# TensorE takes two tiles of the gather-convolution in one step, and VectorE copies out the turned tiles of the odd heads

## The chip, the core and the metric

The kernel runs on one core of a Trainium2 chip, as one program. The metric is the device time of that program in microseconds (us). Engines are named as in the profile: PE (TensorE matmul), PEld (TensorE weight load), ACT (ScalarE), DVE (VectorE), POOL (GpSimd), SP (SyncE, here a DMA queue).

## What is computed

Input x is 16 sequences of 512 tokens with 128 channels. A modulated layer norm gives h; an adaptive gather-convolution with 8 heads and 32 taps is added to x; a second modulated layer norm feeds a mixture of 8 experts with the best 2 chosen; its output is added to x. The change lies in the gather-convolution:

```python
wave = (x @ wave_w.T + wave_b).reshape(Bx, Lx, H, 2)
freq = MIN_FREQ + sigmoid(wave[..., 0]) * (MAX_FREQ - MIN_FREQ)
phase = tanh(wave[..., 1]) * freq
offs = phase[..., None] + freq[..., None] * taps
pos = clip(arange(Lx)[None, :, None, None] + offs, 0.0, Lx - 1)
...
gathered = g0 + frac[..., None] * (g1 - g0)
kmat = (x @ kernel_w.T + kernel_b).reshape(Bx, Lx, H, K)
bins = clip(floor((offs + MAX_RECEPTIVE) / (2.0 * MAX_RECEPTIVE) * K), 0, K - 1)
w = take_along_axis(kmat, bins, axis=3)
y = einsum('blhs,blhsd->blhd', w, gathered).reshape(Bx, Lx, Cx)
```

## The kernel before, in words

**Tiling.** Sequences are taken in 8 pairs (i). In each pair there are 8 rounds (r), one for each residue of the token modulo 8, and in a round 8 heads (h). One head of one round is a tile T of 128 tokens by 512 grid points, so there are 64 rounds (R) and 512 tiles (NT). The kernel does not gather. For each token and each grid point a tile holds a count of taps, got from three matmuls with 32 rows of weights and a relu; it is multiplied by the kernel value of its bin, turned, and multiplied by differences of h.

**One tile, step by step.**
- TensorE, `gap_on` (line 985): a 32-row matmul into `ps_s[T % 4]`. The 32 rows are those of head `T % 4`; four such row groups lie side by side in the array.
- ScalarE, `gap` (line 775): relu on the bank, in place.
- TensorE, `tile_on` (line 990), then `undone_on` (line 994): two more 32-row matmuls added onto the same bank.
- VectorE, `weighted` (line 1303): maximum and product, from the bank into `aw[T % 3]`.
- TensorE, `turn_tile` (line 1000): four 128x128 transposes into one of two banks `ps_t`.
- ScalarE, `tile_evicted` (line 783): copy of that bank to `att[h]`.
- TensorE, `weigh` (line 1020): 32 matmuls on four heads' `att`, twice a round.

**Two banks, one order.** Everything that is turned goes through the two banks `ps_t` in one fixed order, `ORDER` (line 41): the tiles, one `count` a round after head 0, two `edge` units after heads 2 and 4, and in some rounds after heads 6 and 7 the turned h, parameters, steps or second-norm rows. Unit u uses bank `u % 2`, so `unit` (line 891) makes TensorE wait until unit u-2 has been copied out:

```python
u = UNIT[tag]
...
if u >= 2:
    pe.wait_ge(s_ev, u - 1)
return ps_t[u % 2]
```

**The order of work** is written out by hand, one in-order queue for each engine. In the loop over T, TensorE issues `undone_on(T+1)`, `tile_on(T+2)`, `gap_on(T+3)`, then `turn_tile(T)`, then what belongs to the head: `counts` (h 0), `weigh` of the round before (h 1), `turn_edges` (h 2 and 4, line 1007), `bins` (h 3, line 946), `weigh` (h 5), `weigh_edges` (h 7, line 1030), and once in a pair of sequences `waves`, `scores` (line 1052), `ranks` (h 0) and `outputs` (line 1042; h 0 in round 6, h 6 in round 0). ScalarE issues `gap(T+3)`, `tile_evicted(T)`, then its own things for the head: `counted` (h 0, line 767), `edge_evicted` (h 2 and 4, line 790), `copied` (h 3, line 798), and in rounds 1 and 2 the four normalising activations of `centred` (h 1 and 3, line 735). VectorE issues `weighted(T)`, then `edge_terms` (h 2), `binned` (h 5, line 1287) and the norms' and choices' work. `gap_on` waits until VectorE has read tile T-4 out of its bank.

**After the loop** come the last scores and ranks, the scatter of rows to experts, the experts' matmuls (lines 1138 to 1159) and the sums. The change does not touch them.

Of the kernel before, what the change touches and what calls it, by code (L numbers as in the profile page):

```python
# [7 lines left out]
RES = 8  # L8
# [5 lines left out]
NT = PAIRS * TILES  # L14
# [5 lines left out]
ROWS = 32  # L20
QUAD = P // ROWS
KRING = 4
RING = 3
BANKS = 4
SCALE = 2.0 ** 27
GATE = 2.0 ** 90
# [52 lines left out]
UNIT = {tag: n for n, tag in enumerate(ORDER)}  # L79
SIDES = side_order()  # L80
SIDE = {tag: n for n, tag in enumerate(SIDES)}
SLOTS = HEADS + 2
HALF = HEADS // QUAD

# [6 lines left out]
def build(nc, x, wave_wT, wave_b, kern_wT, kern_b, out_wT, w12T, w3T, gateT, cT, wmod,  # L91
# [23 lines left out]
    with ctx:  # L115
# [6 lines left out]
        def sem(name):  # L122
            return ctx.enter_context(nc.semaphore(name))
# [139 lines left out]
        s_kf = sem("end_terms_set")  # L263
        s_n, s_p, s_e = sem("count_added"), sem("gap_product"), sem("gap_ready")
        s_aw, s_at, s_ev, s_y, s_yy = sem("weighted"), sem("turned"), sem("evicted"), sem("y_product"), sem("y_copied")
        s_ga, s_ow, s_xo, s_gc, s_sc = sem("gains_loaded"), sem("out_weights_scaled"), sem("x_new"), sem("h2_ready"), sem("scores_read")
        s_oh, s_gd, s_tg, s_gate = (sem("choice_masks"), sem("score_gap"), sem("gap_tanh"),
                                           sem("gates_in_rows"))
# [224 lines left out]
        def _(pool):  # L493
# [95 lines left out]

            def h_steps(i):  # L590

                pool.wait_ge(s_ev, UNIT["ht", i, 1] + 1)
                if i:
                    pool.wait_ge(s_at, UNIT["dl", i - 1, 1] + 1)
                q = i % 2
                pool.tensor_tensor(dt[:, :, 0:RES - 1, :].rearrange("p b r t -> p r b t"), ht[:, q, 0:RES - 1, :].rearrange("p r (b t) -> p r b t", b=2),
                                   ht[:, q, 1:RES, :].rearrange("p r (b t) -> p r b t", b=2), ALU.subtract)
                pool.tensor_tensor(dt[:, :, RES - 1, 0:HP - 1], rows(ht[:, q, RES - 1, 0:1], [[HP, 2], [1, HP - 1]]),
                                   rows(ht[:, q, 0, 1:2], [[HP, 2], [1, HP - 1]]), ALU.subtract).then_inc(s_dt, 1)
# [109 lines left out]
        def _(act):  # L709
# [93 lines left out]
            for n in range(4):  # L803
                params_turned(0, n)
            counted(0)
            for T in range(BANKS - 1):
                gap(T)
            for b in range(2):
                steps_turned(0, b)
            for T in range(NT):  # L810
                i, R, r, h = T // TILES, T // HEADS, T // HEADS % RES, T % HEADS
                last, more = i - 1, i + 1 < PAIRS
                if T + BANKS - 1 < NT:
                    gap(T + BANKS - 1)
                tile_evicted(T)
                if h == 0 and R + 1 < NR:
                    counted(R + 1)
                if h == 2:
                    edge_evicted(R, 0)
                if h == 3 and R:  # L820
                    copied(R - 1)
                if h == 4:
                    edge_evicted(R, 1)
                if i:
                    if (r, h) in ((2, 1), (2, 3)):
                        centred(1, last, h // 2)
                    if r == 3 and h >= 6:
                        h2_turned(last, h - 6)
                    if (r, h) == (4, 5):
                        gap_tanh(last)  # L830
                if more:
                    if (r, h) in ((1, 1), (1, 3)):
                        centred(0, i + 1, h // 2)
                    if r == 2 and h >= 6:
                        h_turned(i + 1, h - 6)
                    if (r, h) == (3, 3):
                        waves(i + 1)
                    if r == 4 and h >= 6:
                        params_turned(i + 1, h - 6)
                    if r == 5 and h >= 6:  # L840
                        params_turned(i + 1, h - 4)
                    if r == 6 and h >= 6:
                        steps_turned(i + 1, h - 6)
# [34 lines left out]
        def _(pe):  # L878
# [12 lines left out]
            def unit(*tag):  # L891

                u = UNIT[tag]
                assert u == issued[0], (tag, ORDER[issued[0]])
                issued[0] += 1
                if u >= 2:
                    pe.wait_ge(s_ev, u - 1)
                return ps_t[u % 2]

            def aside(*tag):  # L900
# [32 lines left out]
                last.then_inc(s_at, 1)  # L933

            def waves(i):
                pe.wait_ge(s_ev, UNIT["ht", i, 1] + 1)
                bank = aside("wave", i)
                for r in range(RES):
                    last = nc.tensor.matmul(bank[:, r * 16:r * 16 + 16], ht[:, i % 2, r, :], ww[:, :], start=True, stop=True)
                last.then_inc(s_sd, 1)  # L940
# [26 lines left out]
            def counts(R):  # L967
                i, r = R // RES, R % RES
                if r == 0:
                    pe.wait_ge(s_ev, UNIT["ptt", i, 3] + 1)  # L970
                bank = unit("count", R)
                for g in range(2):
                    last = nc.tensor.matmul(bank[:, g * QUAD * EDGES:(g + 1) * QUAD * EDGES], ptt[:, i % 2, 2 * r + g, :], ce[:, :], start=True, stop=True)
                last.then_inc(s_at, 1)
# [12 lines left out]
            def tile_on(T):  # L987
                pe.wait_ge(s_e, T + 1)
                at, params = strip(T)
                nc.tensor.matmul(ps_s[T % BANKS][:, :], params, cn[at, 0, :], start=False, stop=False, skip_group_check=True)  # L990
# [17 lines left out]
                last.then_inc(s_at, 1)  # L1008

            def weigh(R, g):  # L1010
                pe.wait_ge(s_ev, UNIT["tile", HEADS * R + QUAD * g + QUAD - 1] + 1)
                if g == 0:
                    if R % RES == 0:
                        pe.wait_ge(s_ev, UNIT["dl", R // RES, 1] + 1)
                    if R:
                        pe.wait_ge(s_yy, R)
                for j in range(NJ):
                    for k in range(QUAD):
                        h = QUAD * g + k
                        last = nc.tensor.matmul(ps_y[ROWS * k:ROWS * k + ROWS, g * P:g * P + P], dl[:, R // RES % 2, j, h, :],  # L1020
                                                att[:, h, j * P:j * P + P], start=(g == 0 and j == 0), stop=(g == HALF - 1 and j == NJ - 1))
                last.then_inc(s_y, 1)

            def weigh_edges(R, g):
                pe.wait_ge(s_ev, UNIT["edge", R, g] + 1)
                if R % RES == 0 and g == 0:
                    pe.wait_ge(s_hld, 16 * 3 * (R // RES + 1))
                for k in range(QUAD):
                    o = R % RES * 2 * C + QUAD * g + k
                    last = nc.tensor.matmul(ps_y[ROWS * k:ROWS * k + ROWS, g * P:g * P + P], rows(hgr[:, R // RES % 2, o:o + 1], [[HEADS, 2 * D]]),  # L1030
                                            att[:, HEADS + g, k * P:k * P + P], start=False, stop=False)
                last.then_inc(s_y, 1)
# [11 lines left out]
                last.then_inc(s_sd, 1)  # L1044

            def scores(i):
                pe.wait_ge(s_ev, UNIT["h2", i, 1] + 1)
                if i == 0:
                    pe.wait_ge(s_late, NLATE)
                bank = aside("gate", i)  # L1050
                for r in range(RES):
                    last = nc.tensor.matmul(bank[:, r * 8:r * 8 + 8], h2t[:, r, :], gw[:, :], start=True, stop=True)  # L1052
                last.then_inc(s_sd, 1)
# [16 lines left out]
            for n in range(4):  # L1070
                params_turned(0, n)
            counts(0)
            for T in range(BANKS - 1):
                gap_on(T)
            tile_on(0)
            undone_on(0)
            tile_on(1)
            for b in range(2):
                steps_turned(0, b)
            for T in range(NT):  # L1080
                i, R, r, h = T // TILES, T // HEADS, T // HEADS % RES, T % HEADS
                last, more = i - 1, i + 1 < PAIRS
                if T + 1 < NT:
                    undone_on(T + 1)
                if T + 2 < NT:
                    tile_on(T + 2)
                if T + BANKS - 1 < NT:
                    gap_on(T + BANKS - 1)
                turn_tile(T)
                if h == 0 and R + 1 < NR:  # L1090
                    counts(R + 1)
# [90 lines left out]
        def _(dve):  # L1182
# [107 lines left out]
            def weighted(T):  # L1290
# [13 lines left out]
                                                             rows(ks[:, R % 2, h, o:o + 1], [[0, b - a], [1, HP]]), ALU.max, ALU.mult)  # L1304
                ins.then_inc(s_aw, 1)

            def edge_terms(R):

                dve.wait_ge(s_ev, UNIT["count", R] + 1)
                dve.wait_ge(s_kd, R + 1)  # L1310
                if R >= 2:
                    dve.wait_ge(s_est[R % 2], 32 * (R // 2))
                nc.vector.scalar_tensor_tensor(kr[:, R % 2, :], en[:, R % 2, :], -TAPS / 2 * SCALE, kd[:, R % 2, :], ALU.add, ALU.mult).then_inc(s_kr, 1)
# [38 lines left out]
            binned(0)  # L1352
            binned(1)
            edge_terms(0)
            for T in range(NT):
                i, R, r, h = T // TILES, T // HEADS, T // HEADS % RES, T % HEADS
                last, more = i - 1, i + 1 < PAIRS
                weighted(T)
                if h == 2 and R + 1 < NR:
                    edge_terms(R + 1)  # L1360
                if h == 5 and R + 2 < NR:
# [196 lines left out]
```

## Time and profile before

| | |
|---|---|
| median of 3 runs | 1334.32 us |
| runs, lowest to highest | 1331.52 to 1336.67 us |
| the profiled execution's own time | 1336.08 us |
| its span, first to last instruction | 1334.0 us |
| mean granted TensorE clock | 0.956 of full speed |
| busy over the span | PE 86%, PEld 56%, DVE 53%, ACT 69%, POOL 44% |
| the loop over tiles, first to last turned tile | 40.9 to 965.0 us |

The loop over tiles is some 924 of 1334 us; the experts follow from about 1022 us to 1285 us. In the loop the time of a round repeats to a few hundredths of a microsecond, so single pairs of tiles can be read off the timeline and multiplied. Busy time of a matmul is modelled and overlaps the next one; the start of an instruction is what to read. The chain of waits that ended last has little of the loop among its largest parts, so the loop is read from the waits and the timeline.

### The profile page before, as it was taken

To read this page: it belongs to the slowest core of one execution; us is meant where nothing else is said; L and a number is where in the kernel's file an instruction comes from. 1 tells how busy PE (TensorE), PEld (TensorE's weight loads), DVE (VectorE), ACT (ScalarE), POOL (GpSimd) and SP (SyncE) were. 2 spreads that over 40 slices of the span, in tenths; PEclk is the share of its full clock that TensorE was granted. 3 is DMA by queue.
4 is the path that set the end of the run, shared out by engine and by line. 5 is a ranking of instruction groups with operands and counts; after the bars stand their busy time and mean duration, and the time that the engine had idled before them with its cause. 6 is when DMAs were issued, how large, how long until landed. Compare 5 with 4: busy or idle time off the path is not lost. (4 is left out here: it accounts for less than half of the span.)

```text
span 1334.0 us, 34820 instructions
## 1 busy us (share of the span) xinstructions
PE 1141.6 (86%) x11855; PEld 741.1 (56%) x11855; DVE 702.3 (53%) x2252; ACT 916.3 (69%) x1906; POOL 588.1 (44%) x838
## 2 busy tenths in 40 slices
PE   5699999999999999999999999999922989999840
PEld 2366656656665665666566566656621656556520
DVE  4345655564665656566565656556551333333336
ACT  2488887888888788878878888887700555555520
POOL 4133155346436435633643563442436554545520
PEclk9899999999999999999999999999955999999975
DMA  5546446445645544554554455444412442222237
GB/s 181 156 123 175 112 144 162 136 134 165 156 124 167 163 125 140 168 144 121 168 162 127 143 151 138 143 140 116 150 64 68 138 133 72 71 71 71 68 138 262
DMA packets 213178, 179.81 MB, mean 135 GB/s; under 512 B 147600, under 2 KB 183184, under 8 KB 212368
## 3 DMA queue, kind: packets, MB, share of 16 engines
q1 hardware_dynamic: 204336, 159.68, 42.5%
q0 software_dynamic: 8672, 17.92, 4.1%
q8 instruction: 100, 1.64, 0.5%
q14 instruction: 70, 0.57, 0.2%
HBM read 95.42 MB, written 82.12 MB: 133 GB/s over the span
## 5 line engine op out<-in xcount | busy, mean ns | idle before, releaser
L1303 DVE SCALAR_TENSOR_TENSOR aw<-ps,ks 128x64 f32<-128x64 f32 (+7 forms) x960 | 382.0, 437 | 387.4 <-PE ps L994 342.8
L775 ACT ACTIVATE ps<-ps,f 128x512 f32<-128x512 f32 x512 | 343.4, 671 | 131.2 <-PE ps L985 131.2
L1000 PE MATMUL ps<-ident,aw 128*128 128x128 f32 x2048 | 332.9, 285 | 31.6 <-ACT att L783 15.9
L783 ACT ACTIVATE att<-ps 128x512 f32<-128x512 f32 x512 | 310.2, 606 | 11.5 <-PE ps L1000 11.2
L1000 PEld LDWEIGHTS ps<-ident,aw 128*128 128x128 f32 x2048 | 216.3, 141 | 157.9 <-issue 134.4
L604 POOL COPY kn<-kn 128x256 f32<-128x256 f32 x64 | 25.4, 397 | 436.8 <-DVE kn L1287 436.8
L990 PE MATMUL ps<-cn,ptt 32*128 32x512 bf16 x512 | 198.8, 388 | 13.9 <-ACT ps L775 13.9
L994 PE MATMUL ps<-cn,ptt 32*128 32x512 bf16 x512 | 198.7, 388 | 0.0
L985 PE MATMUL ps<-cp,ptt 32*128 32x512 bf16 x512 | 197.9, 389 | 0.0
L705 POOL DMA_INDIRECT y_scratch<-aw,idu x135 | 129.3, 958 | 129.4 <-ACT aw L866 128.1
L853 ACT ACTIVATE ee<-ps 128x256 f32<-128x256 f32 x135 | 51.9, 385 | 152.8 <-PE ps L1144 152.8
L573 POOL DMA_INDIRECT slot_scratch<-hrow,spotu x128 | 127.3, 995 | 48.2 <-issue 33.4
L1144 PE MATMUL ps<-kn,ee 128*128 x270 | 143.0, 612 | 0.0
L1020 PE MATMUL ps<-att,dl 128*32 128x128 f32 x4096 | 140.0, 278 | 0.1
L1450 DVE TENSOR_TENSOR aw<-ee,ps 128x256 f32<-128x256 f32 x135 | 56.9, 421 | 136.4 <-ACT ee L853 135.5
L1020 PEld LDWEIGHTS ps<-att,dl 128*32 128x32 f32 x4096 | 105.1, 110 | 22.2 <-ACT att L790 10.6
L994 PEld LDWEIGHTS ps<-cn,ptt 32*128 32x128 bf16 x512 | 46.4, 91 | 124.6 <-issue 121.2
L1138 PE MATMUL ps<-ident,dl 128*128 128x128 f32 x135 | 38.3, 283 | 55.0 <-DMA dl<-slot_scratch 32.7
L1007 PE MATMUL ps<-ident,ka 128*128 128x128 f32 x512 | 77.3, 274 | 7.8 <-POOL ka L617 7.8
L790 ACT ACTIVATE att<-ps 128x512 f32<-128x512 f32 x128 | 77.9, 608 | 8.3 <-PE ps L1007 8.3
L1159 PE MATMUL ps<-hgr,aw 128*128 x540 | 82.5, 275 | 0.1
L1151 PEld LDWEIGHTS ps<-ident,aw 128*128 128x128 f32 x270 | 38.0, 141 | 71.6 <-issue 46.4
(176 smaller groups left out, 1652.1 us busy)
## 6 DMA issues: line engine op xcount, KB each, us to landing
k_scratch<-kn SPq DMA_DIRECT2D x64, 512.0 KB, 3.5
ka<-e_scratch SPq DMA_DIRECT2D x64, 512.0 KB, 3.2
ks<-k_scratch SPq DMA_DIRECT2D x128, 130.0 KB, 3.3
e_scratch<-kr SPq DMA_DIRECT2D x128, 126.0 KB, 3.4
dl<-slot_scratch SPq DMA_DIRECT2D x135, 65.0 KB, 1.8
att<-y_scratch SPq DMA_DIRECT2D x16, 512.0 KB, 5.2
xc<-in_x SPq DMA_DIRECT2D x8, 512.0 KB, 5.9
h_scratch<-hx SPq DMA_DIRECT2D x16, 256.0 KB, 4.2
```

What stands on the lines that cost most here:

```text
L573: pool.indirect_dma_start(out=slots[:, :], out_offset=bass.IndirectOffsetOnAxis(ap=spotu[:, k * RES + r:k * RES + r + 1], axis=0), in_=hro ...
L705: pool.indirect_dma_start(out=yscr[:, :], out_offset=bass.IndirectOffsetOnAxis(ap=idu[:, s:s + 1], axis=0), in_=yrow[:, y, :], in_offset=N ...
L775: act.activation(ps_s[T % BANKS][:, :], ps_s[T % BANKS][:, :], ACT.Relu, scale=f27[:, i % 2, r, h:h + 1]).then_inc(s_e, 1)
L783: act.activation(att[:, h, :], ps_t[UNIT["tile", T] % 2][:, :], ACT.Copy).then_inc(s_ev, 1)
L985: nc.tensor.matmul(ps_s[T % BANKS][:, :], params, cp[at, :], start=True, stop=True).then_inc(s_p, 1)
L990: nc.tensor.matmul(ps_s[T % BANKS][:, :], params, cn[at, 0, :], start=False, stop=False, skip_group_check=True)
L994: nc.tensor.matmul(ps_s[T % BANKS][:, :], params, cn[at, 1, :], start=False, stop=True, skip_group_check=True).then_inc(s_n, 1)
L1000: last = nc.tensor.transpose(bank[:, j * P:j * P + P], aw[:, T % RING, j * P:j * P + P], ident[:, :])
L1020: last = nc.tensor.matmul(ps_y[ROWS * k:ROWS * k + ROWS, g * P:g * P + P], dl[:, R // RES % 2, j, h, :], att[:, h, j * P:j * P + P], start ...
L1144: nc.tensor.matmul(ps_h[j % 2][:, :], xT[:, j % 2, :], w12[:, bass.ds(experts[j % 8] * (2 * FF), 2 * FF)], start=True, stop=True).then_inc ...
L1159: last = nc.tensor.matmul(ps_z[j % 2][:, 0:C], hidT[:, j % 2, k * P:k * P + P], w3[:, bass.ds(experts[j % 8] * (HALVES * C) + k * C, C)], ...
L1303: ins = nc.vector.scalar_tensor_tensor(dst[:, a:b, :], src[:, a:b, :], -TAPS * SCALE, rows(ks[:, R % 2, h, o:o + 1], [[0, b - a], [1, HP]] ...
```

## The change

TensorE's step covers two tiles. At each even head it issues `tile_on` for T+2 and T+3, `gap_on` for T+4 and T+5, `undone_on` for T+2 and T+3; `turn_tile` and what belongs to a head stay at their heads. ScalarE issues `gap(T+4)` and `gap(T+5)` at each even head ahead of `tile_evicted(T)`, and copies out even heads alone. VectorE issues `weighted(T+2)` in step T, and after it, at odd heads, a copy of the turned tile T to `att[h]`, counted on a semaphore of its own. `aw` has four buffers in place of three. The number of instructions is the same. Who has copied out which unit is kept in the table `EVICTION`, and every wait that asked for a unit's copy now asks for its entry there.

```diff
-RING = 3
+RING = 4
...
+def by_vector(tag):
+
+    return tag[0] == "tile" and tag[1] % 2 == 1
+
+
+def evictions():
+
+    done, counts = [0, 0], {}
+    for tag in ORDER:
+        k = by_vector(tag)
+        done[k] += 1
+        counts[tag] = done[k]
+    return counts
+
+
+EVICTION = evictions()
...
-            for T in range(BANKS - 1):
+            for T in range(BANKS):
                 gap(T)
...
-                if T + BANKS - 1 < NT:
-                    gap(T + BANKS - 1)
-                tile_evicted(T)
+                if h % 2 == 0 and T + BANKS < NT:
+                    gap(T + BANKS)
+                    gap(T + BANKS + 1)
+                if h % 2 == 0:
+                    tile_evicted(T)
...
                 if u >= 2:
-                    pe.wait_ge(s_ev, u - 1)
+                    old = ORDER[u - 2]
+                    pe.wait_ge(s_dv if by_vector(old) else s_ev, EVICTION[old])
...
-                pe.wait_ge(s_ev, UNIT["tile", HEADS * R + QUAD * g + QUAD - 1] + 1)
+                pe.wait_ge(s_ev, EVICTION["tile", HEADS * R + QUAD * g + QUAD - 2])
+                pe.wait_ge(s_dv, EVICTION["tile", HEADS * R + QUAD * g + QUAD - 1])
...
-            for T in range(BANKS - 1):
+            for T in range(BANKS):
                 gap_on(T)
-            tile_on(0)
-            undone_on(0)
-            tile_on(1)
+            for T in range(2):
+                tile_on(T)
+            for T in range(2):
+                undone_on(T)
...
-                if T + 1 < NT:
-                    undone_on(T + 1)
-                if T + 2 < NT:
+                if h % 2 == 0 and T + 2 < NT:
                     tile_on(T + 2)
-                if T + BANKS - 1 < NT:
-                    gap_on(T + BANKS - 1)
+                    tile_on(T + 3)
+                    if T + BANKS < NT:
+                        gap_on(T + BANKS)
+                        gap_on(T + BANKS + 1)
+                    undone_on(T + 2)
+                    undone_on(T + 3)
                 turn_tile(T)
...
+            def tile_evicted(T):
+
+                R, h = T // HEADS, T % HEADS
+                dve.wait_ge(s_at, UNIT["tile", T] + 1)
+                if R:
+                    dve.wait_ge(s_y, weighed(R - 1, "tile", h // QUAD))
+                nc.vector.tensor_copy(att[:, h, :], ps_t[UNIT["tile", T] % 2][:, :]).then_inc(s_dv, 1)
...
+            for T in range(2):
+                weighted(T)
             for T in range(NT):
...
-                weighted(T)
+                if T + 2 < NT:
+                    weighted(T + 2)
+                if h % 2:
+                    tile_evicted(T)
```

## Rows read from the trace of the kernel before

**Rows 1.** The page: busy time, and the clock granted to TensorE in 40 slices.
```profile
PE 1141.6 (86%) x11855; PEld 741.1 (56%) x11855; DVE 702.3 (53%) x2252; ACT 916.3 (69%) x1906; POOL 588.1 (44%) x838
...
PEclk9899999999999999999999999999955999999975
```

**Rows 2.** Waits, 100 to 1000 us: engine line, releaser, us, times, longest.
```profile
DVE aw L1303 <- PE ps L994: 321.3, 307, 2.5
...
PE ps L1000 <- ACT att L783: 15.3, 72, 0.2
```

**Rows 3.** Timeline, heads 0 and 1 of a plain round: start us, us, engine line.
```profile
870.83 0.39 PE L994 MATMUL ps<-cn,ptt 32*128 32x512 bf16 x1
...
871.15 0.42 PEld L1000 LDWEIGHTS ps<-ident,aw 128*128 128x128 f32 x4 [0.23 <-issue]
...
871.30 0.66 ACT L775 ACTIVATE ps<-ps,f 128x512 f32<-128x512 f32 x1 [0.34 <-PE ps L985]
...
871.88 0.59 ACT L783 ACTIVATE att<-ps 128x512 f32<-128x512 f32 x1
...
872.36 0.59 ACT L767 ACTIVATE en<-ps 128x504 int32<-128x504 f32 x1
...
872.58 0.42 PEld L1000 LDWEIGHTS ps<-ident,aw 128*128 128x128 f32 x4 [0.48 <-issue]
```

**Rows 4.** Timeline, heads 2 and 3 of the same round.
```profile
874.19 0.39 PE L994 MATMUL ps<-cn,ptt 32*128 32x512 bf16 x1
...
875.94 0.42 PEld L1000 LDWEIGHTS ps<-ident,aw 128*128 128x128 f32 x4 [0.31 <-issue]
...
877.39 0.39 PE L994 MATMUL ps<-cn,ptt 32*128 32x512 bf16 x1
```

**Rows 5.** Timeline, heads 6 and 7 of the same round, no extra units.
```profile
880.75 0.38 PE L994 MATMUL ps<-cn,ptt 32*128 32x512 bf16 x1
...
882.25 0.42 PEld L1000 LDWEIGHTS ps<-ident,aw 128*128 128x128 f32 x4 [0.23 <-issue]
...
883.44 0.39 PE L994 MATMUL ps<-cn,ptt 32*128 32x512 bf16 x1
```

**Rows 6.** Timeline, heads 6 and 7 of a round with extra units.
```profile
491.32 0.39 PE L994 MATMUL ps<-cn,ptt 32*128 32x512 bf16 x1
...
493.07 0.42 PEld L1000 LDWEIGHTS ps<-ident,aw 128*128 128x128 f32 x4 [0.31 <-issue]
...
494.86 0.38 PE L994 MATMUL ps<-cn,ptt 32*128 32x512 bf16 x1
```

**Rows 7.** Timeline, heads 0 and 1 of a round with scores at head 0.
```profile
451.08 0.39 PE L994 MATMUL ps<-cn,ptt 32*128 32x512 bf16 x1
...
452.11 1.85 PE L1052 MATMUL ps<-gw,h2t 128*128 128x8 f32 x16
...
455.82 0.39 PE L994 MATMUL ps<-cn,ptt 32*128 32x512 bf16 x1
```

**Rows 8.** Timeline, heads 2 and 3 of a round with normalising activations.
```profile
539.96 0.38 PE L994 MATMUL ps<-cn,ptt 32*128 32x512 bf16 x1
...
543.94 0.38 PE L994 MATMUL ps<-cn,ptt 32*128 32x512 bf16 x1
...
544.03 1.69 ACT L735 ACTIVATE hrow<-xo,shift,rstd 128x128 f32<-128x128 f32 x4
```

**Rows 9.** Busy by stretch: heads 4 and 5 of that round; a stretch after scores.
```profile
543.94:548.50 4.56, 3.69 (x51) 2.37 (x51) 2.10 (x5) 4.40 (x10) 2.72 (x4) 1.00 0.57 217
...
570.00:573.00 3.00, 3.00 (x42) 2.09 (x39) 2.27 (x13) 1.26 (x2) 1.07 (x1) 0.53 0.62 112
```

**Rows 10.** Timeline, the same matmul at half the clock.
```profile
572.81 0.60 PE L994 MATMUL ps<-cn,ptt 32*128 32x512 bf16 x1
```

**Rows 11.** Timeline, VectorE: a sum out of PSUM, and `weighted`.
```profile
870.46 0.68 DVE L1320 TENSOR_TENSOR xo<-ps,xc 128x512 f32<-128x512 f32 x1
...
874.61 0.76 DVE L1303 SCALAR_TENSOR_TENSOR aw<-ps,ks 128x64 f32<-128x64 f32 x2 [0.88 <-PE ps L994]
```

More of the change, by code:

```diff
@@ L265, in build @@
         s_aw, s_at, s_ev, s_y, s_yy = sem("weighted"), sem("turned"), sem("evicted"), sem("y_product"), sem("y_copied")
+        s_dv = sem("tile_evicted_by_vector")
         s_ga, s_ow, s_xo, s_gc, s_sc = sem("gains_loaded"), sem("out_weights_scaled"), sem("x_new"), sem("h2_ready"), sem("scores_read")
@@ L590, in h_steps @@
             def h_steps(i):
-                pool.wait_ge(s_ev, UNIT["ht", i, 1] + 1)
+                pool.wait_ge(s_ev, EVICTION["ht", i, 1])
                 if i:
@@ L935, in waves @@
             def waves(i):
-                pe.wait_ge(s_ev, UNIT["ht", i, 1] + 1)
+                pe.wait_ge(s_ev, EVICTION["ht", i, 1])
                 bank = aside("wave", i)
@@ L969, in counts @@
                 if r == 0:
-                    pe.wait_ge(s_ev, UNIT["ptt", i, 3] + 1)
+                    pe.wait_ge(s_ev, EVICTION["ptt", i, 3])
                 bank = unit("count", R)
@@ L1010, in weigh @@
             def weigh(R, g):
-                pe.wait_ge(s_ev, UNIT["tile", HEADS * R + QUAD * g + QUAD - 1] + 1)
+                pe.wait_ge(s_ev, EVICTION["tile", HEADS * R + QUAD * g + QUAD - 2])
+                pe.wait_ge(s_dv, EVICTION["tile", HEADS * R + QUAD * g + QUAD - 1])
                 if g == 0:
                     if R % RES == 0:
-                        pe.wait_ge(s_ev, UNIT["dl", R // RES, 1] + 1)
+                        pe.wait_ge(s_ev, EVICTION["dl", R // RES, 1])
                     if R:
@@ L1024, in weigh_edges @@
             def weigh_edges(R, g):
-                pe.wait_ge(s_ev, UNIT["edge", R, g] + 1)
+                pe.wait_ge(s_ev, EVICTION["edge", R, g])
                 if R % RES == 0 and g == 0:
@@ L1046, in scores @@
             def scores(i):
-                pe.wait_ge(s_ev, UNIT["h2", i, 1] + 1)
+                pe.wait_ge(s_ev, EVICTION["h2", i, 1])
                 if i == 0:
@@ L1305, in weighted @@
                 ins.then_inc(s_aw, 1)
+            def tile_evicted(T):
[4 more added lines that the diff above has]
+                nc.vector.tensor_copy(att[:, h, :], ps_t[UNIT["tile", T] % 2][:, :]).then_inc(s_dv, 1)
             def edge_terms(R):
-                dve.wait_ge(s_ev, UNIT["count", R] + 1)
+                dve.wait_ge(s_ev, EVICTION["count", R])
                 dve.wait_ge(s_kd, R + 1)
```

## The prediction, made before the changed kernel had run

> **What bounds the kernel now.** First the page [rows 1]: TensorE is the busiest engine, 86% of the span, and in the loop its granted clock is full. That looks like a loop bound by TensorE alone, but busy time of matmuls is modelled, so the waits come next [rows 2]. VectorE waits 321.3 us of the loop for TensorE; TensorE hardly records waits for the copies (15.3 us). Then the timeline of one plain round, which shows how near those copies are.
>
> Take heads 0 and 1 [rows 3] and count from the moment the three 32-row matmuls start. Tile 0 is turned at +0.32. ScalarE's relu starts at +0.47, its copy of tile 0 0.58 later, at +1.05, and lasts 0.59, to +1.64. Tile 1 is turned at +1.75, 0.11 after that. Between tile 0 and tile 1 only `count` goes through the two banks, so tile 1 needs tile 0's bank. The idle ahead of tile 1's loads is 0.48 where it was 0.23 ahead of tile 0's: TensorE already waits 0.25 there. The pair is over at +3.36 [rows 3, 4], 1.61 behind tile 1's turning. Heads 2 and 3 are alike [rows 4]: tile 3 at +1.75, end at +3.20. An `edge` unit makes tile 3 use tile 2's bank, and in the same way tile 5 uses tile 4's. Between tiles 6 and 7 nothing goes through the banks in a plain round: tile 7 needs tile 5's bank, long free, and the pair takes 2.69 [rows 5].
>
> So the loop is bound by a chain through two engines: strips, relu, copy, next turning.
>
> **What the change does to that chain.** In an even step ScalarE now has two relus ahead of the copy of tile T, and that copy is still ScalarE's, since T is even. The relus cannot run earlier, as their `gap_on` matmuls are issued in the same step. VectorE's new copies are those of odd tiles, which do not hold these three turnings.
>
> Step by step: relu T+4 at +0.47, relu T+5 at +1.05, copy at +1.63, its end at +2.22, tile T+1 turned at +2.33. That is 1.75 plus 0.58. What follows (1.61 for heads 0, 1 and 4, 5; 1.45 for heads 2, 3) is unchanged, so **each such pair grows by 0.58**. The distance from one relu to the next is not in the trace: below, 0.48, as from a copy to ScalarE's next operation [rows 3]; above, 0.66, a whole relu. I take 0.58, the distance from a relu to a copy, as the relu is what it times.
>
> TensorE's own work shrinks. Two blocks of strips with 0.32 each become one. In it `tile_on` and `gap_on` cover four row groups and `undone_on` comes a second time to two of them, so it costs one more stream: 0.22, the difference between this matmul at half and at full clock, 0.60 and 0.38 [rows 5, 10]. The block takes 0.54 (bounds 0.32, all six side by side, and 0.64, nothing gained). Where TensorE sets the time this and one lost switch from strips to full-height matmuls (idle 0.23 [rows 3]) matter; where ScalarE's copy sets it, they are swallowed by the wait.
>
> **Heads 6 and 7, plain.** Tile 7 is not held. 0.54 of strips, 0.42 for the loads of four transposes, and the 1.19 behind tile 7's turning [rows 5] make 2.15 where 2.69 was: **0.54 less**. The next `gap_on` needs VectorE: its first product starts 0.42 behind a strip [rows 4, 11], here at +0.64, and two of 0.76 end at +2.16. That is just in time, so there is nothing more to gain.
>
> **Heads 6 and 7 with extra units** (turned h, parameters, steps, second norm; rounds 2 to 6). An extra unit stands between tiles 6 and 7, which makes tile 7 wait for tile 6's copy by ScalarE: +1.75 now [rows 6], +2.33 then, and 1.79 behind it: 4.12 for 3.54, **0.58 more**.
>
> **Pairs with long work at head 0** (waves, scores, outputs) or outputs at head 6. TensorE sets these: scores alone take 1.85, more than ScalarE's chain needs, and the pair 4.74 [rows 7]. They lose 0.10 of strips and some 0.2 of a switch: **0.3 less**.
>
> **Rounds 1 and 2, normalising activations.** These four activations (1.69 [rows 8]) make the next relu late, so those pairs are long now: 3.98 [rows 8] at heads 2, 3 and 4.56 [rows 9] at heads 4, 5. Their delay fits into the time ScalarE will then wait: behind the `count` copy at +2.11 they begin at +2.6 and end at +4.3, before the next relu is due (3.94 plus 0.47). Heads 2, 3 come to 3.78: 0.2 less. Behind head 3 there is `copied` ahead of them; they end about 0.3 after the relu is due at 3.78 plus 0.47, so heads 4, 5 come to some 4.2: 0.4 less.
>
> **VectorE's copies.** 128x512 out of PSUM by VectorE is not in the trace. ScalarE's copy (0.59) and VectorE's sum out of PSUM (0.68 [rows 11]) bound it; I take 0.65. It waits for turning T+1 (+2.33 and about 0.66 for the last transpose), runs to +3.65, and the next `weighted` is ready only at 3.94 plus 0.64. It hides, with 0.9 to spare. Banks that wait for it (`edge`, `count`, extra units) come 0.9 or more later. The fourth `aw` buffer keeps `weighted(T+2)` from waiting for a turning; it costs nothing. No DMA is added, and SP and POOL, which follow the products' semaphores, keep their order.
>
> **The sum.** Of the 256 pairs of tiles, by the conditions in the code: 128 are held by ScalarE's copy and plain (41 at heads 0, 1; 47 at 2, 3; 40 at 4, 5), 128 x 0.58 = +74.2. 35 with extra units, +20.3. 21 plain at heads 6, 7, -11.3. 29 with long work, -8.7. 14 and 14 behind normalising activations, -2.8 and -5.6. The other 15 (start, choices in round 4, last sequences) at zero. In all **+66 us**. The profiled execution took 1336.08 us, 1.8 above the median of the runs; the sum there is 1402, and against the median 1334.3 + 66 = **1400 us**, slower by 5%.
>
> **Rivals.**
>
> *TensorE's saving comes through (faster).* It is one mechanism: VectorE shares the copies, ScalarE is lighter by 256 copies, and no turning waits. For it speaks that ScalarE is the second busiest engine [rows 1]. Every pair would then lose what a plain last pair loses: 256 x 0.54 = 138, 1196 us. It decides if tile T's copy is over before TensorE reaches tile T+1, at about +1.4. Against it stands the order: the copy cannot start before +1.05 even if the second relu cost nothing, and ends at +1.64. I give it 0.05. The Trainium skill, TensorEngine Tiling (Array Packing), section PSUM Bottleneck, advises to use both ScalarE and VectorE to empty PSUM; by that rule alone the time would be this rival's. It speaks of throughput, and the trace here shows a latency.
>
> *The clock drops.* TensorE's own work in a held pair is some 3.0 of 3.94, 76%. The nearest row is the pair at heads 4, 5 of a normalising round, 3.69 busy of 4.56, 81%, at clock 1.00 [rows 9]. But after scores, whose matmuls stream 8 columns each, the clock was 0.53 [rows 9]. If a quarter of the pairs ran at half the clock with 2.0 more each, that is 64 x 2.0 = 128: 1530 us. I give it 0.08. The Trainium skill, TensorE: Matmul & The Clock Gate, section "A second HAM failure mode: psum-queue depth-cycling", tells of a kernel whose small idle spells between groups on changing banks made the clock swing; by it this rival would be likely. In this trace small waits have not done it.
>
> *VectorE becomes late.* A copy that waits at the head of its queue keeps the next product back. It decides if the copy ends later than 4.58, 0.9 more than worked out. With 0.3 lost in each of 192 pairs that gives 58 more, 1460 us. 0.04.
>
> *No change that can be measured.* A measurement of this kernel tells about 0.5%, 7 us. It would take a distance between relus near 0.15, against every row: 0.03.
>
> **How the numbers follow.** Forecast 0.80. Relu to relu 0.48 to 0.66 moves 163 pairs by -16 to +13; the block of strips -11 to +5 in the 50 pairs that TensorE sets; four row groups at once may bring the first relu up to one stream, 0.22, later in 163 pairs: +36. That is 1373 to 1454; with the odd pairs, and as the three will not all fall on one side, the range is 1365 to 1445. Faster 0.05, within 0.5% 0.03, slower 0.92.
>
> **What would show it.** In a plain round: TensorE's second turning at +2.33 at heads 0, 2 and 4, and an idle of about 0.9 ahead of it, laid to ScalarE's copy (line 783's successor); TensorE's recorded waits for that copy up from 15 us to over 100; rounds near 13.8 where 12.6 was; the last pair at 2.15. I am wrong if the two relus stand closer than 0.45, if the clock in the loop is below 0.95, or if most of TensorE's idle time is laid to VectorE.

## The result, and the profile after

The changed kernel took 1409.3 us (median of 4 runs, 1408.7 to 1410.2) beside 1335.0 us for the kernel before: 1.0555 times as long, interval 1.0541 to 1.0569. Forecast were 1400 us and a range of 1365 to 1445. All times here and below are of undisturbed runs, which in the last variant leaves out one of four, of 2109 us.

The page of the changed kernel: engines' busy time, and the clock granted to TensorE in 40 slices.

```profile
PE 1094.2 (78%) x11855; PEld 716.3 (51%) x11855; DVE 860.3 (61%) x2508; ACT 790.2 (56%) x1650; POOL 589.0 (42%) x838
...
PEclk9999999999999999999999999999985899999985
```

Against [rows 1] ScalarE's work has moved to VectorE (ACT 69% to 56%, DVE 53% to 61%), TensorE's share fell from 86% to 78%, and the mean clock stayed where it was (0.956 before, 0.959 now). No engine is fuller than TensorE was, and yet the kernel is slower: a matter of waits.

Its waits from 100 to 1000 us: who waited for whom, us in total, times, longest.

```profile
PEld ps L1022 <- DVE aw L1329: 163.8, 167, 1.6
...
PE ps L1022 <- ACT att L802: 141.5, 181, 1.4
...
DVE aw L1329 <- PE ps L1016: 95.9, 120, 1.8
```

Line 1022 is the turning of a tile, 802 ScalarE's copy, 1329 `weighted`. TensorE's matmuls waited 15.3 us for that copy before [rows 2] and wait 141.5 us now. The weight loads of the same turnings are put down to VectorE (163.8 us), which is the releaser that the profile happens to find for the load. The timeline settles which it is. Heads 0 and 1, then 2 and 3, of a round (start us, us, engine line; VectorE's one row here is the products of tiles 2 and 3):

```profile
420.29 0.39 PE L1012 MATMUL ps<-cn,ptt 32*128 32x512 bf16 x2
...
420.30 0.75 PE L1007 MATMUL ps<-cp,ptt 32*128 32x512 bf16 x2
...
420.73 1.24 ACT L794 ACTIVATE ps<-ps,f 128x512 f32<-128x512 f32 x2 [0.41 <-PE ps L1007]
...
421.13 1.28 DVE L1329 SCALAR_TENSOR_TENSOR aw<-ps,ks 128x512 f32<-128x512 f32 x2
...
421.88 0.60 ACT L802 ACTIVATE att<-ps 128x512 f32<-128x512 f32 x1
...
422.36 0.60 ACT L786 ACTIVATE en<-ps 128x504 int32<-128x504 f32 x1
...
422.63 0.63 PE L1022 MATMUL ps<-ident,aw 128*128 128x128 f32 x4 [0.77 <-ACT att L802]
...
424.20 0.39 PE L1012 MATMUL ps<-cn,ptt 32*128 32x512 bf16 x2
...
424.42 0.38 PE L1016 MATMUL ps<-cn,ptt 32*128 32x512 bf16 x2
...
424.63 1.24 ACT L794 ACTIVATE ps<-ps,f 128x512 f32<-128x512 f32 x2 [1.67 <-PE ps L1007]
...
425.79 0.60 ACT L802 ACTIVATE att<-ps 128x512 f32<-128x512 f32 x1
...
426.53 0.63 PE L1022 MATMUL ps<-ident,aw 128*128 128x128 f32 x4 [0.71 <-ACT att L802]
...
427.95 0.39 PE L1012 MATMUL ps<-cn,ptt 32*128 32x512 bf16 x2
```

In the first pair the two relus start at 420.73 and the copy of tile 0 only at 421.88, 1.15 behind the first relu where it was 0.58 behind before [rows 3]. Tile 1 is turned at 422.63, 0.15 after that copy ends. In the second pair the strips start at 424.20, tile 3's matmuls at 426.53, and the pair ends at 427.95: 3.75 where [rows 4] had 3.20. VectorE's product of tile 3 was over at 422.41, four microseconds before its turning, so it did not hold it; ScalarE's copy of tile 2, over at 426.39, did. `undone_on` (line 1016) starts 0.22 behind `tile_on` (line 1012), the one stream expected.

The pair at heads 6 and 7 of another round, with extra units, by the same view:

```profile
463.21 0.39 PE L1012 MATMUL ps<-cn,ptt 32*128 32x512 bf16 x2
...
465.52 0.42 PEld L1022 LDWEIGHTS ps<-ident,aw 128*128 128x128 f32 x4 [0.92 <-DVE aw L1329]
465.55 0.63 PE L1022 MATMUL ps<-ident,aw 128*128 128x128 f32 x4 [0.71 <-ACT att L802]
...
467.30 0.39 PE L1012 MATMUL ps<-cn,ptt 32*128 32x512 bf16 x2
```

The second turning is at +2.31 and the pair lasts 4.09, where [rows 6] had +1.75 and 3.54. Here the load's idle is laid to VectorE and the matmul's to ScalarE, 0.03 apart: the same wait.

One thing more, which no mean over the loop shows: the granted clock fell to half in four short stretches of the loop. Three of them are in round 2, the fourth in round 5 of the last sequences. Round 2 of two pairs of sequences, first without such a stretch, then with it (the third number from the end is the clock), and the row that stands ahead of the second:

```profile
458.00:460.50 2.50, 2.28 (x16) 0.97 (x14) 1.80 (x5) 2.50 (x8) 1.27 (x1) 1.00 0.52 98
583.00:585.50 2.50, 2.50 (x10) 0.99 (x10) 0.69 (x1) 2.40 (x6) 1.60 (x2) 0.50 0.54 103
```

```profile
582.16 0.81 PE L1029 MATMUL ps<-ident,ka 128*128 128x128 f32 x4 [1.58 <-POOL ka L636]
```

In both TensorE had just waited 1.58 for GpSimd's part of the edge unit. Experiment 4 says where that wait comes from.

### The profile page after: what moved, and what is told of

Same layout as the page of the kernel before. It is cut to its first block, busy times and chain, and to the rows that moved or that the text cites. A ratio compares the mean times of both kernels' runs of the same rounds, so it can differ in the third digit from the quotient of the medians.

```text
span 1408.1 us, 34896 instructions
## 1 busy us (share of the span) xinstructions
PE 1094.2 (78%) x11855; PEld 716.3 (51%) x11855; DVE 860.3 (61%) x2508; ACT 790.2 (56%) x1650; POOL 589.0 (42%) x838
## 4 chain that ended last, share of the span: by engine, by line
PE 54%; ACT 16%; issue 15%; POOL 7%; DVE 4%; DMA 3%; SPq 1%; POOLq 0%; DVEq 0%; ACTq 0%
PE ps L1022 12%; PE ps L1043 9%; PE ps L1170 8%; ACT att L802 7%; ACT ps L794 6%; PE ps L1012 5%; PE ps L1185 4%; PE ps L968 3%; PE ps L1053 2%; PE ps L1065 2%; PE ps L1177 2%; DMA att<-y_scratch 2%; PE ps L1164 1%; POOL y_scratch L724 1%; POOL rstd L534 1%
## 5 line engine op out<-in xcount | busy, mean ns | idle before, releaser
L794 ACT ACTIVATE ps<-ps,f 128x512 f32<-128x512 f32 x512 | 317.3, 658 | 292.5 <-PE ps L1007 292.4
L1022 PE MATMUL ps<-ident,aw 128*128 128x128 f32 x2048 | 327.9, 285 | 153.9 <-ACT att L802 152.4
L1329 DVE SCALAR_TENSOR_TENSOR aw<-ps,ks 128x64 f32<-128x64 f32 (+7 forms) x960 | 366.8, 433 | 130.7 <-PE ps L1016 105.8
L1339 DVE COPY att<-ps 128x512 f32<-128x512 f32 x256 | 176.3, 689 | 173.6 <-PE ps L1022 172.9
L802 ACT ACTIVATE att<-ps 128x512 f32<-128x512 f32 x256 | 153.3, 599 | 3.7 <-issue 1.9
L1007 PE MATMUL ps<-cp,ptt 32*128 32x512 bf16 x512 | 106.0, 391 | 4.7 <-DVE aw L1329 4.7
L1012 PE MATMUL ps<-cn,ptt 32*128 32x512 bf16 x512 | 101.4, 390 | 0.7 <-ACT ps L794 0.7
L1016 PE MATMUL ps<-cn,ptt 32*128 32x512 bf16 x512 | 98.1, 378 | 0.0
L809 ACT ACTIVATE att<-ps 128x512 f32<-128x512 f32 x128 | 77.8, 608 | 10.6 <-PE ps L1029 10.6
```

Of the source, the lines that this page charges most:

```text
L794: act.activation(ps_s[T % BANKS][:, :], ps_s[T % BANKS][:, :], ACT.Relu, scale=f27[:, i % 2, r, h:h + 1]).then_inc(s_e, 1)
L802: act.activation(att[:, h, :], ps_t[UNIT["tile", T] % 2][:, :], ACT.Copy).then_inc(s_ev, 1)
L1007: nc.tensor.matmul(ps_s[T % BANKS][:, :], params, cp[at, :], start=True, stop=True).then_inc(s_p, 1)
L1022: last = nc.tensor.transpose(bank[:, j * P:j * P + P], aw[:, T % RING, j * P:j * P + P], ident[:, :])
L1329: ins = nc.vector.scalar_tensor_tensor(dst[:, a:b, :], src[:, a:b, :], -TAPS * SCALE, rows(ks[:, R % 2, h, o:o + 1], [[0, b - a], [1, HP]] ...
L1339: nc.vector.tensor_copy(att[:, h, :], ps_t[UNIT["tile", T] % 2][:, :]).then_inc(s_dv, 1)
```

## The experiments

All are compared with the kernel before, measured on the same chip in the same sitting (medians 1334 to 1336 us). The changed kernel was timed in a sitting of its own. A pair of tiles is counted from its block of strips to the next one, a round from the block at its head 0 to that of the next round; the eight pairs of sequences are numbered from 0.

**Theory.** In 163 of 256 pairs of tiles the turning of tile T+1 waits for ScalarE's copy of tile T; the second relu stands ahead of that copy and is paid in full. **Rivals.** VectorE's copies hold the loop; a step of two tiles costs TensorE something by itself; the loop pays for ScalarE's load, not for its order.

**1. The copy between the relus.**

```diff
-                if h % 2 == 0 and T + BANKS < NT:
-                    gap(T + BANKS)
-                    gap(T + BANKS + 1)
                 if h % 2 == 0:
+                    if T + BANKS < NT:
+                        gap(T + BANKS)
                     tile_evicted(T)
+                    if T + BANKS < NT:
+                        gap(T + BANKS + 1)
```

> The changed kernel with ScalarE's order in an even step made relu T+4, copy of tile T, relu T+5 (before this: both relus, then the copy). Theory (the second relu ahead of the copy holds the turning of T+1): the copy starts at +1.24, when tile T has been turned, and the second turning comes at +1.95 where it was +2.3; held pairs fall from 3.91 and 3.76 to about 3.55 and 3.4, the pair with extra units from 4.09 to 3.7, the plain last pair grows from 2.16 to about 2.4 as the late relu now holds the next strips. 163 x -0.36 and 21 x +0.27 give -53: about 1356 us. Rival (VectorE's copies hold the loop): unchanged, 1409. Rival (a step of two tiles costs by itself on TensorE): unchanged, 1409.

Measured: 1358.3 us, ratio 1.0176 (1.0159 to 1.0193). Moving one ScalarE instruction gives back 51 of the 74 us. Plain held pairs fall to 3.54 and 3.39, as expected; the last pair stays at 2.16, where 2.4 was expected. One held pair (heads 6 and 7 of round 4, with extra units), strips, relu, copy, relu, turning, next strips:

```profile
472.79 0.39 PE L1013 MATMUL ps<-cn,ptt 32*128 32x512 bf16 x2
...
473.23 0.66 ACT L794 ACTIVATE ps<-ps,f 128x512 f32<-128x512 f32 x1 [0.99 <-PE ps L1008]
...
474.02 0.60 ACT L802 ACTIVATE att<-ps 128x512 f32<-128x512 f32 x1
...
474.51 0.66 ACT L794 ACTIVATE ps<-ps,f 128x512 f32<-128x512 f32 x1
...
474.73 0.42 PEld L1023 LDWEIGHTS ps<-ident,aw 128*128 128x128 f32 x4 [0.70 <-issue]
...
476.26 0.39 PE L1013 MATMUL ps<-cn,ptt 32*128 32x512 bf16 x2
```

The copy is at +1.23, the turning at +1.94, and the pair takes 3.47 where the changed kernel has 3.83. Both rivals that said 1409 are out as the main cause.

**2. The pairs kept, all copies by ScalarE.** The same with `by_vector` false for every tile and `tile_evicted(T)` by ScalarE at each head.

> The changed kernel, but ScalarE copies out all tiles again, the odd ones after the even ones; step of two tiles kept. Theory: held pairs stay at 3.91 and 3.76, since the copy of T stands where it stood; the normalising activations of rounds 1 and 2 start later by a copy and delay 28 pairs by 0.8 to 1.3 each: 1425 to 1440 us. Rival (VectorE's copies are the cost): back to 1350 or below.

Measured: 1426.2 us, 1.0687 (1.0669 to 1.0705). The step of two tiles does the harm without VectorE; VectorE's copies are worth 17 us in it, nearly all beside the normalising activations (12.4 in round 1 and 3.6 in round 2, added up from the two traces). Plain held pairs are at 3.91 and 3.76, as in the changed kernel.

**3. A step of one tile, odd tiles by VectorE.** The order of the kernel before on TensorE and ScalarE; VectorE issues `weighted(T+1)`, then its copy of an odd tile T.

> The kernel before with its step of one tile, but VectorE copies out the odd tiles (aw with four buffers, VectorE one tile ahead of its copy). Theory: held pairs as before, 3.36 and 3.20, as tile T's copy keeps one relu ahead of it; only pairs behind the normalising activations gain, 14 x 0.7 and 14 x 0.9: 1313 to 1325 us, faster than the kernel before. Rival (VectorE's copies are the cost): slower than 1335.

Measured: 1360.7 us, 1.0200 (1.0172 to 1.0228), **a miss**, slower where a gain was expected. Plain pairs at heads 0 to 5 are as expected and round 1 gains 0.96 us (14.70 to 13.74). But round 4 loses 2.1 to 3.6 (0.9 in pair 4 of sequences, where the kernel before has a stretch at half the clock), round 5 0.2 to 1.5 and round 2 0.7 to 1.5; over the traces that is 14.3, 5.1 and 6.3 us, against 6.5 gained in round 1; the last pair of round 7, 3.20 for 2.69, loses 3.5 more. In round 4 VectorE has the experts' choices to make. Its row there, with the turning that waits, then the next turning:

```profile
470.58 0.75 DVE L1325 SCALAR_TENSOR_TENSOR aw<-ps,ks 128x256 f32<-128x256 f32 x2
...
471.25 0.68 DVE L1335 COPY att<-ps 128x512 f32<-128x512 f32 x1
...
471.85 0.68 DVE L1309 TENSOR_TENSOR kn<-ps,kbias 128x512 f32<-128x512 f32 x1
...
473.44 0.96 DVE L1378 TENSOR_TENSOR both<-oh 128x64 bf16<-128x64 f32 x1
474.32 1.40 DVE L1325 SCALAR_TENSOR_TENSOR aw<-ps,ks 128x256 f32<-128x256 f32 x4
...
475.12 0.42 PEld L1021 LDWEIGHTS ps<-ident,aw 128*128 128x128 f32 x4 [2.53 <-DVE aw L1325]
475.12 0.66 PE L1021 MATMUL ps<-ident,aw 128*128 128x128 f32 x4 [2.23 <-DVE aw L1325]
...
477.81 1.11 PE L1021 MATMUL ps<-ident,aw 128*128 128x128 f32 x4
```

Copy, bias add and masks (up to line 1378) stand in one row ahead of the next product, and TensorE's matmuls wait 2.2 us, its loads 2.5. In the kernel before, the same turning waited for VectorE too, 0.74 and 1.03. The next four transposes take 1.11 where these took 0.66. The clock says why (second stretch; the third number from the end is the granted clock):

```profile
474.00:477.00 3.00, 1.88 (x23) 1.31 (x24) 2.42 (x6) 0.00 (x0) 0.89 (x4) 0.80 0.68 239
477.00:479.00 2.00, 2.00 (x13) 1.24 (x11) 0.76 (x2) 1.28 (x3) 0.00 (x0) 0.50 0.51 172
```

After the wait TensorE ran at half the clock, 1.2 GHz, until the next round had begun. So VectorE's copies are not free. In the step of two tiles they cost nothing in rounds 4 and 5, which take 16.03 and 15.56 with them (the changed kernel) and without them (experiment 2).

**4. VectorE's bias add ahead of its copy.** In the changed kernel, `binned(R + 2)` at head 5 moved before `tile_evicted(T)`.

> The changed kernel with VectorE's bias add of the kernel values (binned, head 5) put ahead of its copy of tile 5. Theory: in round 2 the turning of the first edge unit waits for GpSimd, whose row of work starts with that add, now behind a copy that waits for a turning; heads 2 and 3 of round 2 fall from 4.65 toward 3.76 and nothing else moves: 7 x 0.9, so 1402 to 1404 us. Rival (the round-2 wait comes from elsewhere): unchanged, 1409.

Measured: 1394.9 us, 1.0447 (1.0430 to 1.0465). Right in kind, short in size: 14 us, not 6. Round 2 falls from 17.21 to 15.83 in pairs 1, 2 and 3 of sequences (heads 2 and 3 from 4.66 to 3.76, heads 4 and 5 from 4.56 to 4.07), and from 18.20 to 15.83 in pairs 4, 5 and 6, where heads 2 and 3 had taken 6.1 to 6.2 with the half clock. Round 5 of the last sequences, the fourth place of half clock, gives 1.7 back. No stretch of this run's loop is at half the clock. The row of waits in the changed kernel, from VectorE's copy to TensorE's edge unit:

```profile
447.02 0.69 DVE L1339 COPY att<-ps 128x512 f32<-128x512 f32 x1 [0.30 <-PE ps L1022]
447.63 0.68 DVE L1313 TENSOR_TENSOR kn<-ps,kbias 128x512 f32<-128x512 f32 x1
...
448.38 0.40 POOL L623 COPY kn<-kn 128x256 f32<-128x256 f32 x1 [5.52 <-DVE kn L1313]
...
456.03 0.68 POOL L636 TENSOR_SCALAR ka<-kn 128x8 f32<-128x8 f32 x1
...
456.76 0.42 PEld L1029 LDWEIGHTS ps<-ident,ka 128*128 128x128 f32 x4 [1.82 <-POOL ka L636]
```

The copy waits for a turning, the bias add for the copy, GpSimd for the bias add, and GpSimd's operation for the edge unit stands behind the inverse deviations and half a norm, all in one queue. TensorE pays nine microseconds later.

**5 and 6. A small operation ahead of the copy, and behind it.**

```diff
                 if h % 2 == 0:
+                    act.activation(extra[:, T // 2 % 8, :], ident[:, 0:64], ACT.Copy)
                     tile_evicted(T)
```

> The changed kernel with one small ScalarE copy (128x64, SBUF to a buffer of its own) more in each even step, between the second relu and the copy of tile T. Theory (whatever stands on ScalarE between the relus and the copy is paid in full in the 163 held pairs): with some 0.2 us for such an operation each held pair grows by 0.2, from 3.91 to 4.1 and 3.76 to 3.95; the plain last pair stays at 2.16: +33, about 1442 us. Rival (ScalarE's copy is waited for but TensorE or VectorE is the bound): less than a third of it.

> The same small ScalarE copy put behind the copy of tile T. Theory: ScalarE has room there, nothing moves but the pairs behind the normalising activations: 1409 to 1415 us. Rival (the loop pays for ScalarE's load, not for its order): the same +33 as with the operation ahead of the copy.

Measured: ahead 1432.1 us, 1.0735 (1.0716 to 1.0755), so 23 us more than the changed kernel; behind 1407.8 us, 1.0549 (1.0530 to 1.0568), so nothing. The operation lasts 0.25 but moves the next one by 0.15, and held pairs grow by just that, 3.91 to 4.05 and 3.75 to 3.90. That 163 x 0.15 is 24 is in part luck: in the trace 186 pairs grow, by 26.5 us together, and some 5 come back because neither of these two runs has the changed kernel's stretches of half clock. The size expected was off by my 0.2. ScalarE does the same work in both, so its load is not what is paid: the place is.

**7. The turning first.** TensorE turns tile T ahead of the strips, ScalarE copies it ahead of both relus, VectorE adds the bias ahead of its copy.

```diff
+                turn_tile(T)
                 if h % 2 == 0 and T + 2 < NT:
                     tile_on(T + 2)
...
-                turn_tile(T)
...
-                if h % 2 == 0 and T + BANKS < NT:
-                    gap(T + BANKS)
-                    gap(T + BANKS + 1)
                 if h % 2 == 0:
                     tile_evicted(T)
+                    if T + BANKS < NT:
+                        gap(T + BANKS)
+                        gap(T + BANKS + 1)
```

> Step of two tiles, but TensorE turns tile T ahead of the strips, ScalarE copies it ahead of both relus, and VectorE's bias add stands ahead of its copy of tile 5. Theory: tile T's copy is over at about +1.4, before TensorE comes to tile T+1 at +1.5, so no turning waits: plain pairs 3.13, 3.03, 3.2 and 2.31, a plain round 11.7 where the kernel before had 12.6; less in rounds 4 and 5, where VectorE has the choices to make: 1270 to 1300 us, faster than both kernels. Rival (pairs cost by themselves, or VectorE's copies do): slower than 1335.

Measured: 1340.1 us (ten runs, 1336.5 to 1350.9; the trace is of one at 1336.5), 1.0066 (1.0037 to 1.0095). The plain pairs are near what was worked out, 3.04, 3.05, 3.16 and 2.31, and a plain round takes 11.6 us, 1.0 less than before. The total is **a miss**: rounds 2, 4 and 5 are long (up to 16.2, 17.3 and 15.1, where the kernel before has 15.4, 15.4 and 13.3), those that experiment 3 had made long. They and the pairs behind long work take the whole gain. Some 11 us of it are the clock's: four rounds 2 and four rounds 5 hold a stretch at half the clock, behind a wait of 1.8 to 2.0 us, and take 16.2 and 15.1 where the others take 15.0 and 13.6.

**8. The turning first, all copies by ScalarE.**

> As the kernel with the turning first, but ScalarE copies out all tiles. Theory: ScalarE then has two relus and two copies in a pair of some 3.1 and still keeps tile T's copy first, so plain rounds stay near 11.7 to 12; VectorE's choices in rounds 4 and 5 cost less, normalising activations in rounds 1 and 2 more: 1270 to 1310 us. If VectorE's copies are worth having it is slower than the one beside it.

Measured: 1319.8 us, 0.9894 (0.9876 to 0.9912), **faster than both kernels**, by 1.1% than the one before, but outside the 1270 to 1310 expected. Plain rounds stay at 11.56; beside experiment 7, round 4 takes 15.6 for 17.3 and round 5 13.7 for 13.6 or 15.1; round 1, beside the normalising activations, 14.0 for 13.0. From 60 us on its loop has no stretch at half the clock. Waits, 100 to 940 us:

```profile
ACT att L802 <- PE ps L1021: 117.2, 185, 1.8
...
PE ps L1021 <- ACT att L802: 17.0, 28, 1.2
```

Now ScalarE waits for the turning; the turning's matmuls wait for ScalarE's copy 17.0 us, where the changed kernel has 141.5 up to 1000 us. The whole gain is 15 us, far from 64 rounds at 1.0: against the kernel before, heads 2 and 3 lose 0.5 to 0.9 in rounds 3 to 6, and rounds 3 to 6 gain nothing as a whole.

**9 and 10. VectorE's copies only where ScalarE is full.** `by_vector` true for odd heads of round 1; then for heads 1 and 3 of rounds 1 and 2.

> As the kernel with the turning first and all copies by ScalarE, but in round 1 of each pair of sequences, where ScalarE has eight normalising activations, VectorE copies the odd tiles. Theory (a copy belongs on the engine that has time in that round): round 1 falls from 14.0 to 13.05, as in the kernel whose odd copies are all VectorE's, and the other rounds stay: 7 x 0.97 less, about 1313 us. Rival (the order alone made the gain, the engine does not matter): 1320.

> As before, but VectorE copies the tiles of heads 1 and 3 alone, in rounds 1 and 2, those directly ahead of ScalarE's normalising activations. Theory: round 1 at 13.05 to 13.3 and round 2 some 0.3 to 1.0 shorter than 14.3, with no copy of VectorE's ahead of its bias add at head 5: 1307 to 1313 us. Rival (VectorE's copies in round 2 make GpSimd's row of work late again): 1315 to 1325.

Measured: 1318.2 us, 0.9867 (0.9848 to 0.9886), and 1316.8 us, 0.9848 (0.9824 to 0.9872). **Both expectations were missed**; the second time lies in its rival's range. Round 1 falls from 14.0 to 13.04 as expected. But round 2 rises from 15.12 to 15.6 (three pairs of sequences) or 16.2 to 16.3 (three) in the first variant, and to 16.2 or 16.3 in two of six in the second. The rival's wait is there: in round 2 the edge unit waits 2.0 us for GpSimd, where it waited 1.5 in experiment 8. And the rounds of 16.2 and 16.3 are exactly those where the clock was at half behind that wait. The first variant, just behind the wait, in a pair of sequences without and in one with half clock:

```profile
419.00:421.50 2.50, 2.50 (x19) 1.38 (x18) 0.24 (x2) 2.50 (x7) 1.75 (x2) 1.00 0.54 103
305.00:307.50 2.50, 2.50 (x7) 1.02 (x6) 0.00 (x0) 2.41 (x7) 1.25 (x1) 0.50 0.50 97
```

The interval of the first variant overlaps that of experiment 8, from which it is not told apart, and that of the second variant.

## Why the prediction was right

The time was inside the range, 9 us above the forecast. The mechanism, ScalarE's second relu ahead of the copy that holds the next turning, is shown by experiments 1, 5 and 6. By its own steps:

- **The held pairs** (+0.58): measured 3.91, 3.76 and 3.91 for 3.36, 3.20 and 3.36, so +0.55, and 4.09 for 3.54 with extra units. The distance between relus, assumed, is 0.58: the copy comes 1.16 behind the first relu. The 0.03 less is the first relu, at +0.43 where it was at +0.47. A round of three such pairs and a plain last pair takes 13.73 for 12.61, near the 13.8 forecast.
- **Extra units in round 4** (+0.58) **failed**: in six pairs of sequences this last pair took 3.83, for 4.07 in most of them, so it became shorter by 0.24. The forecast added 0.58 to all 35 such pairs as if each took the 3.54 of [rows 6]. In round 4 the pair was held by VectorE, whose choices made a product late: the loads of tile 6's turning waited 1.03 for it. In the changed kernel the products are made two tiles ahead and that wait is gone.
- **The plain last pair** (-0.54): 2.16 for 2.69. The second stream of `undone_on` starts 0.22 behind, and four row groups at once delay the first relu by nothing; the upper bound on that was not needed.
- **Long work at head 0** (-0.3): 4.53 for 4.74, so -0.2; outputs at head 6 4.26 for 4.38, -0.1. A little over-priced.
- **Pairs beside the normalising activations** (-0.2 and -0.4): round 1 as forecast (3.76 for 4.04, 4.14 for 4.62). **Round 2 failed**: at heads 2 and 3 4.66 for 3.98, and 6.1 to 6.2 in the three pairs of sequences with half clock; at heads 4 and 5 4.56, unchanged, and 4.0 to 4.1 in those three. The step that failed is the sentence on VectorE's copies, "It hides, with 0.9 to spare", and that POOL keeps its order. The order holds, but I asked only whether the next product is late and not what else stands behind the waiting copy. That is the bias add that starts GpSimd's row of work. Experiment 4 prices it at 14 us, the half clock behind the wait included.
- **The sum is near in part by luck.** Added up pair by pair, the loop grew by 74.4 us between the two traces, where the terms forecast 66.1. Heads 2 to 5 of round 2 grew by 6.8 where -4.2 was forecast, 11.0 too much; the 35 pairs with extra units grew by 14.6, where 20.3 was forecast, most of the difference in round 4. These two errors have opposite signs; what is left of all other terms is 3.
- **The clock**: 0.959 over the span, 0.99 from 100 to 1034 us, so above the 0.95 that would have shown the forecast wrong. TensorE's waits of 0.7 to 0.9 in each pair did not halve it, and a quarter of the pairs at half clock, which was the rival, did not come. But the clock did fall to half in four short stretches (two before the change, in round 4), three of them right behind a wait of 1.58 for the edge unit. They cost some 1.0 us in each of those three rounds (18.2 for 17.2) and 1.5 in the fourth place (6.39 for 4.90 in experiment 4), 4 to 5 us in all. The Trainium skill, TensorE: Matmul & The Clock Gate, section "A second HAM failure mode: psum-queue depth-cycling", would have made that rival likely. For the small idle spells of nearly every pair the trace does not show it; three of its four falls stand behind a longer wait, the fourth behind waits of 0.70, 0.28 and 0.34 in one pair.
- **The sign by the profile's labels**: "if most of TensorE's idle time is laid to VectorE". For the weight loads it is so laid (163.8 us), and read by the label alone this sign would have spoken against a forecast that the timeline bears out.
- **TensorE's saving comes through**: this rival needed the copy of tile T before +1.4. With the order that meets it (experiment 7) plain rounds fall by 1.0. So it was the right condition, and the given order ruled it out. Its 1196 us were out of reach even so: at 0.54 a pair a round would lose 2.2, and what the copies cost VectorE in rounds 2, 4 and 5 was left out.
- **Both engines empty PSUM**, as the Trainium skill, TensorEngine Tiling (Array Packing), section PSUM Bottleneck, advises: in the two-tile step it saves 17 us (experiment 2 beside the changed kernel), in the one-tile step it costs 26 us (experiment 3), with the turning first 20 us (experiments 7 and 8). Which engine has room in which round decides.

Left open: why the same wait is followed by half the clock in some pairs of sequences and not in others; and how the lateness that is left in rounds 2, 4 and 5 of experiment 7 divides between GpSimd's row and VectorE's, which no run separated. The four longer of its ten runs (1346.9 to 1350.9) have no profile.

## What to carry to other kernels

When steps are merged to save an engine's own work, list for each shared buffer the one operation that frees it, and count what its engine now does ahead of it: here one relu, 0.58 us in two of three steps, was dearer than everything that the merge saved, and putting the freeing copy first, with all copies left to ScalarE, turned a loss of 5.6% into a gain of 1.1%. Before work is moved to an engine with a low mean share, look at the rounds where it is full, and at everything that stands behind an instruction that will wait, down to the queues that it feeds. Read the clock in the stretch behind each long wait and not over the loop: the mean of 0.99 hid what made rounds of the same work differ by 1.0 to 1.5 us.

## What the runs showed of the hardware that was not expected

- A ScalarE operation that lasts 0.25 us (128x64) sets the next one back by 0.15 only; relus that last 0.66 are 0.58 apart, copies of 0.60 are 0.48 apart. The distance to the next start is the price, not the recorded duration.
- VectorE's copy of 128x512 out of PSUM takes 0.68 to 0.69 us, where ScalarE's takes 0.60.
- TensorE's granted clock stayed at 1.00 through pairs with a wait of 0.7 to 0.9 us each, but fell to 0.50 behind some single longer waits and not behind others of the same length. Of the six edge units of round 2 that waited, it fell behind none at 1.5 us (experiment 8), three at 1.6 (changed kernel), two at 1.7 (experiment 1), three at 1.8 (experiment 3), and four, three and two at 2.0 (experiments 7, 9 and 10). With the 2.2 us of experiment 3 in round 4 it fell in all seven.
